# Rounded squares from ScalarE, the MLP input rounded from PSUM, a new order of work, and split products for q and k

## The reference

```python
x = x + conv31x31_depthwise(group_norm(x)) + bias
x = x + window_block(group_norm(x))

def window_block(x):            # windows of 7x7 tokens, shifted by 3
    t = windows(roll(x, (-3, -3)))                       # N, 49, 96
    h = ln(t) * ln1_s + ln1_b
    q, k, v = h @ wq + bq, h @ wk + bk, h @ wv + bv      # 12 heads of 8
    a = softmax(q k^T / sqrt(8))
    t = t + (a v) @ wo + bo
    h = ln(t) * ln2_s + ln2_b
    t = t + gelu(h @ w1 + b1) @ w2 + b2                  # 96 -> 384 -> 96
    return roll(unwindow(t), (3, 3))
```

## Time and profile before

| what | value |
|---|---|
| median of 3 runs | 5947.31 us (5946.79 to 5955.28) |
| profiled execution, its own time | 5965.81 us |
| its span, first to last instruction | 5964.0 us |
| mean granted TensorE clock | 0.976 of full speed |
| busy share of the span: PE, PEld | 94%, 74% |
| DVE, ACT, POOL | 62%, 58%, 64% |

### The profile page before, as it was taken

The page is one execution under the profiler, slowest core; times in us unless marked ns, Lnnn a source line. Parts: engine busy times, 40 slices in busy tenths (PEclk is TensorE's granted clock), DMA queues, the critical chain, the costliest instruction groups (busy, mean ns, idle before and its releaser), DMA issues.

```text
span 5964.0 us, 233920 instructions
## 1 busy us (share of the span) xinstructions
PE 5586.8 (94%) x100144; PEld 4428.8 (74%) x100144; DVE 3678.1 (62%) x6074; ACT 3454.9 (58%) x4952; POOL 3802.2 (64%) x4822
## 2 busy tenths in 40 slices
PE   6999999999959999999999999999999999999998
PEld 6999999999946666666666666666666666666665
DVE  2222222222227777777777777777777777777774
ACT  3444444444336666666666666666666666666665
POOL 2222222222247888887878888888888888788875
PEclk9999999999959999999999999999999999999997
DMA  4444444444335666666666666666666666666662
GB/s 110 108 106 106 106 107 107 106 107 106 82 84 126 140 137 136 137 139 132 137 133 139 135 138 138 138 136 136 139 138 137 135 138 138 132 138 137 134 134 58
DMA packets 1099836, 740.86 MB, mean 124 GB/s; under 512 B 465429, under 2 KB 1070709, under 8 KB 1098709
## 3 DMA queue, kind: packets, MB, share of 16 engines
q1 hardware_dynamic: 1069620, 687.18, 51.8%
q0 software_dynamic: 29184, 38.71, 2.7%
HBM read 409.02 MB, written 316.46 MB: 122 GB/s over the span
## 4 chain that ended last, share of the span: by engine, by line
POOL 34%; issue 17%; PE 8%; DVE 7%; ACT 5%; POOLq 0%; DVEq 0%; ACTq 0%
POOL b_mid_hi L715 6%; POOL b_outs L780 5%; POOL b_mid_lo L722 5%; POOL b_sq_lo L761 4%; POOL b_t_lo L754 4%; POOL b_sq_lo L729 3%; POOL b_t L745 3%; DVE b_y L990 3%; ACT b_lg L802 3%; DVE b_h L975 2%; ACT b_rstd L807 2%; PE ps_ring L1037 2%; POOL b_t_hi L750 2%; DVE b_vd L983 1%; POOL b_mx_planes L789 1%
## 5 line engine op out<-in xcount | busy, mean ns | idle before, releaser
L223 POOL TENSOR_SCALAR xn<-xin,aff 96x896 f32<-96x896 f32 x192 | 233.9, 1218 | 1207.9 <-DVE aff L330 1195.2
L1092 PEld LDWEIGHTS ps_pv<-b_vd,b_probs_t 128*64 128x64 f32 x24576 | 772.5, 140 | 163.8 <-issue 154.8
L908 DVE TENSOR_REDUCE b_mx<-ps_s 113x12 f32<-113x588 f32 x1024 | 783.4, 765 | 174.7 <-PE ps_s L1046 173.9
L815 ACT ACTIVATE b_probs_t<-ps_t 128x588 f32<-128x588 f32 x1024 | 666.9, 651 | 332.1 <-PE ps_t L1046 306.4
L417 PE MATMUL ps_conv<-toep_hi,blocks_hi 128*128 128x304 f32 (+5 forms) x4032 | 844.2, 291 | 0.0
L417 PE MATMUL ps_conv<-toep_hi,blocks_lo 128*128 128x304 f32 (+5 forms) x4032 | 839.1, 290 | 0.0
L417 PE MATMUL ps_conv<-toep_lo,blocks_hi 128*128 128x304 f32 (+5 forms) x4032 | 838.0, 289 | 0.0
L1092 PE MATMUL ps_pv<-b_vd,b_probs_t 128*64 128x18 f32 x24576 | 824.0, 213 | 0.4 <-issue 0.3
L722 POOL TENSOR_TENSOR b_mid_lo<-b_mid,b_mid_hi 128x392 fp32r<-128x392 f32 x768 | 789.8, 1028 | 22.0
L353 DVE SCALAR_TENSOR_TENSOR x1t<-ps_conv,biasb,xin 128x896 f32<-128x896 f32 x96 | 110.5, 1151 | 1024.4 <-PE ps_conv L417 1024.4
L780 POOL TENSOR_TENSOR b_outs<-b_y,b_xs 96x392 f32<-96x392 f32 x256 | 317.7, 1241 | 524.8 <-DVE b_y L990 524.8
(11 more groups left out here) (145 smaller groups left out, 12574.1 us busy)
## 6 DMA issues: line engine op xcount, KB each, us to landing
stacked_qk<-b_planes SPq DMA_DIRECT2D x512, 220.5 KB, 2.9
b_q_st<-stacked_qk SPq DMA_DIRECT2D x512, 220.5 KB, 4.4
b_k_st<-stacked_qk SPq DMA_DIRECT2D x512, 220.5 KB, 5.7
toep<-filters_padded SPq DMA_DIRECT2D x96, 936.5 KB, 6.9
stacked_qk<-b_planes SPq DMA_DIRECT2D x512, 147.0 KB, 2.3
stacked_qk<-b_planes SPq DMA_DIRECT2D x512, 73.5 KB, 1.9
b_xs<-x_scratch SPq DMA_DIRECT2D x224, 147.0 KB, 2.8
out<-b_outs SPq DMA_DIRECT2D x224, 147.0 KB, 3.2
```

What stands on the lines that cost most here:

```text
L815: act.activation(pt[:, p, 0:HEADS * TOK].rearrange("k (e n) -> k e n", e=2), ps_t[:, :, 0:HPAIR * TOK], ACT.Exp, scale=float(DH) ** -0.5). ...
L908: dve.tensor_reduce(mx[0:rows_q, :].rearrange("q (e m p) -> q e m p", e=2, p=PAIRS)[:, :, :, p], ps_s[0:rows_q, :, 0:HPAIR * TOK].rearrang ...
L1092: ins = pe.matmul(to, pt[:, p, at:at + WS], vd[:, m % VR, p, h, :, :], start=True, stop=True, skip_group_check=True)
```

## The change

1. ACT makes the rounded squares. sq1_hi and sq2_hi are written by a second Square of ACT from ps_xc; the two DVE casts go. 2. sq2_lo is subtracted by DVE, behind row_max 3, no longer by POOL. 3. h2_hi is a product that DVE reads from PSUM, ahead of h2; the cast goes. 4. The maxima's middle plane goes from DVE to POOL, as a tensor_scalar behind the output's addition and copy. 5. q and k: h1 is made twice by DVE (h1_hi, h1), then h1_lo; the weights are split once; each product is three float32r matmuls instead of one in float32, and waits for h1_lo. 6. New order: on POOL the wrap copy stands ahead of mid_hi 0, and mid_hi 1 ahead of t0; on PE below_max 2 stands between scores 1 and w1c.

```diff
@@ POOL
                 if qkv is not None:
                     pool.wait_ge(S["sq1_high"], qkv + 1)
+                    pool.wait_ge(S["sq1"], qkv + 1)
                     pool.tensor_tensor(sq1_lo[:, :], sq1[:, :], sq1_hi[:, :].bitcast(F32), ALU.subtract)
-                mid_high(mlps, 0, i)
...
                     pool.tensor_copy(xs[:, gn % XS, :, HW:XW], xs[:, gn % XS, :, 0:SHIFT])
+                mid_high(mlps, 0, i)
                 mid_low(mlps, 0)
+                mid_high(mlps, 1, i)
...
-                mid_high(mlps, 1, i)
                 mid_low(mlps, 1)
                 mid_high(mlps, 2, i)
-                if proj is not None:
-                    pool.wait_ge(S["sq2_high"], proj + 1)
-                    pool.tensor_tensor(sq2_lo[:, :], sq2[:, :], sq2_hi[:, :].bitcast(F32), ALU.subtract)
                 mid_low(mlps, 2)
...
+                if att is not None:
+                    pool.wait_ge(S["mx_rest"], att + 1)
+                    pool.tensor_scalar(mx_planes[:, 1, :, :], mx_rest[:, :, :], 1.0, 0.0, ALU.mult, ALU.add)
@@ ACT
+                if qkv is not None:
+                    square(i, qkv, sq1_hi, "xc1", "sq1_high", "sq1_split", 1.0 / C, "var1")
                 if qkv is not None:
                     square(i, qkv, sq1, "xc1", "sq1", "sq1_split", 1.0 / C)
...
                     after(act, i, "h2_done", qkv - (PROJ - QKV))
+                    after(act, i, "h2_high", qkv - (PROJ - QKV))
...
                 if proj is not None:
                     square(i, proj, sq2, "xc2", "sq2", "sq2_split")
+                if proj is not None:
+                    square(i, proj, sq2_hi, "xc2", "sq2_high", "sq2_split", used="var2")
@@ DVE
+            dve.memset(h1_hi[:, :].bitcast(F32), 1.0)
+            dve.memset(h1_lo[:, :].bitcast(F32), 0.0)
...
+            dve.tensor_copy(wqk_hi[:, :, :], wqk[:, :, :]).then_inc(S["wprep"], 1)
+            dve.wait_ge(S["wprep"], 6)
+            dve.tensor_tensor(wqk_lo[:, :, :], wqk[:, :, :], wqk_hi[:, :, :].bitcast(F32), ALU.subtract)
...
-                if qkv is not None:
-                    high(i, qkv, sq1_hi, sq1, "sq1", "var1", 1, "sq1_high")
...
                     dve.wait_ge(S["rstd1"], qkv + 1)
+                    after(dve, i, "k_ps", qkv)
+                    dve.scalar_tensor_tensor(h1_hi[0:C, :], ps_xc[0:C, 0:NT], 1.0 / C, rstd[:, :], ALU.mult, ALU.mult)
                     after(dve, i, "v_ps", qkv)
                     dve.scalar_tensor_tensor(h1[0:C, :], ps_xc[0:C, 0:NT], 1.0 / C, rstd[:, :], ALU.mult, ALU.mult)
+                    dve.wait_ge(S["h1_high"], qkv + 1)
+                    dve.wait_ge(S["h1_done"], qkv + 1)
+                    dve.tensor_tensor(h1_lo[0:C, :], h1[0:C, :], h1_hi[0:C, :].bitcast(F32), ALU.subtract)
                 row_max(i, att, 3)
                 if proj is not None:
-                    high(i, proj, sq2_hi, sq2, "sq2", "var2", 1, "sq2_high")
+                    dve.wait_ge(S["sq2_high"], proj + 1)
+                    dve.wait_ge(S["sq2"], proj + 1)
+                    dve.tensor_tensor(sq2_lo[:, :], sq2[:, :], sq2_hi[:, :].bitcast(F32), ALU.subtract)
...
+                    dve.wait_ge(S["rstd2"], proj + 1)
+                    after(dve, i, "w1_ps", NM * proj)
+                    after(dve, i, "h2_split", proj)
+                    dve.tensor_tensor(h2_hi[:, :], ps_xc[0:C, 0:NT], rstd[:, :], ALU.mult)
...
                     dve.tensor_tensor(h2[:, :], ps_xc[0:C, 0:NT], rstd[:, :], ALU.mult)
-                if proj is not None:
-                    high(i, proj, h2_hi, h2, "h2_done", "w1_ps", NM, "h2_high")
...
-                if att is not None:
-                    dve.wait_ge(S["mx_rest"], att + 1)
-                    dve.tensor_copy(mx_planes[:, 1, :, :], mx_rest[:, :, :]).then_inc(S["mx_mid"], 1)
@@ PE
                     after(pe, i, "h2_done", qkv - (PROJ - QKV))
+                    after(pe, i, "h2_high", qkv - (PROJ - QKV))
...
                 scores(i, att, 1)
+                below_max(i, soft, 2)
                 expand(i, s, mlps, 2, "w1c")
...
-                below_max(i, soft, 2)
                 scores(i, att, 2)
...
-                    pe.wait_ge(S["h1_done"], qkv + 1)
-                    product(i, s, "q", wqk[:, 0, :], h1[:, :], C, "q_ps")
+                    pe.wait_ge(S["h1_split"], qkv + 1)
+                    wait_bank(pe, i, s, "q")
+                    to = bank(i, s, "q")[0:C, 0:NT]
+                    pe.matmul(to, wqk_hi[:, 0, :], h1_hi[:, :], start=True, stop=False)
+                    pe.matmul(to, wqk_lo[:, 0, :], h1_hi[:, :], start=False, stop=False)
+                    pe.matmul(to, wqk_hi[:, 0, :], h1_lo[:, :], start=False, stop=True).then_inc(S["q_ps"], 1)
```

More of the change, by code:

```diff
@@ L498, in window_pass @@
         h1 = sb("h1", [C + 1, NT])
+        h1_hi = sb("h1_hi", [C + 1, NT], F32R)
+        h1_lo = sb("h1_lo", [C + 1, NT], F32R)
+        wqk_hi = sb("wqk_hi", [C + 1, 2, C], F32R)
+        wqk_lo = sb("wqk_lo", [C + 1, 2, C], F32R)
         h2 = sb("h2", [C, NT])
@@ L535, in window_pass @@
                  "pv_ps rden_done o_done ot_ps ot_done wo_ps t1_done xc2 sq2 var2 lg2 rstd2 h2_done w1_ps gelu_done "
-                 "w2_ps y_done added out_done sq1_high sq1_split sq2_high sq2_split h2_high h2_split").split()
+                 "w2_ps y_done added out_done sq1_high sq1_split sq2_high sq2_split h2_high h2_split h1_high h1_split").split()
         S = {n: sem("b_" + n) for n in names}
@@ L781, in step @@
                                        ALU.add).then_inc(S["added"], 1)
+                if att is not None:
+                    pool.wait_ge(S["mx_rest"], att + 1)
+                    pool.tensor_scalar(mx_planes[:, 1, :, :], mx_rest[:, :, :], 1.0, 0.0, ALU.mult, ALU.add).then_inc(
+                        S["mx_mid"], 1)
                 if mlps is not None:
@@ L816, in exps, with square @@
                                ps_t[:, :, 0:HPAIR * TOK], ACT.Exp, scale=float(DH) ** -0.5).then_inc(S["exp_done"], 1)
-            def square(i, n, dst, src, done, split, scale=1.0):
+            def square(i, n, dst, src, done, split, scale=1.0, used=None):
                 act.wait_ge(S[src], n + 1)
                 after(act, i, split, n)
+                if used:
+                    after(act, i, used, n)
                 act.activation(dst[:, :], ps_xc[0:C, 0:NT], ACT.Square, scale=scale).then_inc(S[done], 1)
@@ L910, in row_max @@
                                   ALU.max).then_inc(S["mx_done"], 1)
[L912 to L915, removed]
             def step(i, s):
@@ L945, in step @@
                     dve.wait_ge(S["rstd1"], qkv + 1)
+                    after(dve, i, "k_ps", qkv)
+                    dve.scalar_tensor_tensor(h1_hi[0:C, :], ps_xc[0:C, 0:NT], 1.0 / C, rstd[:, :], ALU.mult,
+                                             ALU.mult).then_inc(S["h1_high"], 1)
                     after(dve, i, "v_ps", qkv)
@@ L948, in step @@
                                              ALU.mult).then_inc(S["h1_done"], 1)
+                    dve.wait_ge(S["h1_high"], qkv + 1)
+                    dve.wait_ge(S["h1_done"], qkv + 1)
+                    dve.tensor_tensor(h1_lo[0:C, :], h1[0:C, :], h1_hi[0:C, :].bitcast(F32), ALU.subtract).then_inc(
+                        S["h1_split"], 1)
                 row_max(i, att, 3)
                 if proj is not None:
-                    high(i, proj, sq2_hi, sq2, "sq2", "var2", 1, "sq2_high")
+                    dve.wait_ge(S["sq2_high"], proj + 1)
+                    dve.wait_ge(S["sq2"], proj + 1)
+                    dve.tensor_tensor(sq2_lo[:, :], sq2[:, :], sq2_hi[:, :].bitcast(F32), ALU.subtract).then_inc(
+                        S["sq2_split"], 1)
                 if qkv is not None:
@@ L973, in step @@
                     dve.wait_ge(S["rstd2"], proj + 1)
+                    after(dve, i, "w1_ps", NM * proj)
+                    after(dve, i, "h2_split", proj)
+                    dve.tensor_tensor(h2_hi[:, :], ps_xc[0:C, 0:NT], rstd[:, :], ALU.mult).then_inc(S["h2_high"], 1)
+                if proj is not None:
+                    dve.wait_ge(S["rstd2"], proj + 1)
                     after(dve, i, "h2_split", proj)
                     dve.tensor_tensor(h2[:, :], ps_xc[0:C, 0:NT], rstd[:, :], ALU.mult).then_inc(S["h2_done"], 1)
-                if proj is not None:
-                    high(i, proj, h2_hi, h2, "h2_done", "w1_ps", NM, "h2_high")
                 if qkv is not None:
@@ L1135, in step @@
                 if qkv is not None:
-                    pe.wait_ge(S["h1_done"], qkv + 1)
-                    product(i, s, "q", wqk[:, 0, :], h1[:, :], C, "q_ps")
-                if qkv is not None:
-                    pe.wait_ge(S["h1_done"], qkv + 1)
-                    product(i, s, "k", wqk[:, 1, :], h1[:, :], C, "k_ps")
+                    pe.wait_ge(S["h1_split"], qkv + 1)
[4 more added lines that the diff above has]
```

(8 more changed lines are left out.)

10 lines of the change are left out of this document (7 added, 3 removed).

## The result

The changed kernel is slower: median 6097.48 us (6080.36 to 6124.23, 4 runs) against 5950.94 us, a ratio of 1.0249 with a 95% interval of 1.0212 to 1.0286. The forecast was 5847 us, faster. Most stretches of the new order came out within a quarter of a microsecond of what it said, but it missed two things: what a gap on PE does to PE's clock, and one PSUM bank.

The account below looks back on a forecast made before the run. Bound: the loop var2, ln, exp, h2, h2_hi, v copies, y, POOL's addition and queue to sq2_lo. 3.97 + 11.75 = 15.72 a step against 16.11, 0.39 x 256 = 100 us less, gave 5847 us; range 5760 to 5955.

Parts of the forecast that it names:

- var2 to y: Stretch on DVE from PE's var2 to y: 4.81 us before, 3.97 forecast with h2_hi made from PSUM, saving 0.84.
- y to POOL's mid_lo: Stretch on POOL from y to mid_lo of plane 1, now with mx_mid on POOL: 8.45 us forecast.
- var2 to h1_lo: Stretch over PE, ACT and DVE from var2 until h1_lo is ready: 12.95 us forecast, 8.98 after y.
- The lock: DVE subtractions with two SBUF inputs wait for a running POOL instruction; h1_lo, ready at 8.98, ends at 9.88 after y.
- the list of signs: Signs of being right: period 15.6 to 15.9, h1_lo rows 0.9 to 1.3, PE waiting at q, not var2.
- case C: Rival: waiting h1_lo also lets POOL's next mid_hi pass; 16.23 a step, 5978 us, slower; chance 0.15.
- DVE's subtractions for q and k stand behind sq2_lo ...; POOL's idle takes that up: DVE's subtractions and POOL's planes come some 0.5 us later after xc2; POOL's idle 1.99 before the addition absorbs it.
- case A: Main case: h1_lo waits for POOL's mid_lo, sq2_lo's wait is hidden; 15.72 us a step; chance 0.59.
- the lock missed: Rival B: neither DVE subtraction meets a POOL instruction; 15.51 us a step, 5793 us; chance 0.14.
- PE alone would allow 15.16 ...: neither is the bound: PE's own work would allow 15.16 us a step, POOL's 12.95; ACT's way to h1 and the lock bind instead.
- The rounded products: On PE, six rounded passes for q and k instead of four float32 ones: 0.16 us less a step.

Follow-up runs that it names:

- e2_no_rest_q: The changed kernel without DVE's remainder of q, so q's PSUM bank is free once ACT has read it; ratio 1.0074.
- e6_fill_xc2: The changed kernel with 3 unread matmuls on PE ahead of its wait at xc2 alone; ratio 1.0034.
- e1_qk_whole: The changed kernel with part five undone: q and k one float32 product each, no h1_hi or h1_lo; 5913.99 us, ratio 0.9903.
- e10_real_work_in_gap: The changed kernel with below_max 3 (24 matmuls) moved on PE from behind k to ahead of xc2; ratio 1.0037.
- e12_before_gap_two: The kernel before with two unread products ahead of h1 on DVE; 6273.15 us, ratio 1.0506.
- e4_before_gap: The kernel before with one unread product ahead of h1 on DVE; ratio 1.0036.
- e7_fill_var2: The changed kernel with 4 unread matmuls on PE ahead of its wait at var2 alone; 6283.69 us, ratio 1.0510.

## Why the prediction was wrong, point by point

- **var2 to y: right.** Forecast 3.97, measured 3.95 (2168.13 to 2172.08). The cast's hidden wait for POOL was real and is gone.
- **y to POOL's mid_lo: right within 0.25.** Forecast 8.45; with a period of 16.16 the mid_lo at 2164.13 stands 8.21 after y. mx_mid's row is 0.27 and stands where POOL was idle behind the addition before.
- **var2 to h1_lo: right.** Forecast 12.95, measured 12.89.
- **The lock: right in kind.** h1_lo ends 0.42 after mid_lo's row (2165.57 against 2165.15), sq2_lo too (2167.50 against 2167.08), where 0.40 was forecast from the conv pass. It cost less, since h1_lo arrived near mid_lo's end: its row is 0.71, not 0.9 to 1.3, and q started 0.73 after xc2, undelayed. PE did not wait at q for h1_lo, as the list of signs had it. The section "Who interferes with whom" of the Trainium skill's page "SBUF — State Buffer" is borne out by both rows. It is so in the whole window pass: where h1_lo (204 of 237 instances) or sq2_lo (215 of 237) starts beside a running POOL instruction, it ends 0.41 to 0.46 after that one. Behind h1_lo, POOL's next instruction ends 0.38 or more after h1_lo in all 204, so POOL never passes it. The mechanism of case C, DVE losing the lock twice, does not occur.
- **"DVE's subtractions for q and k stand behind sq2_lo ...; POOL's idle takes that up": the first step that failed.** It asked who waits for the remainders on POOL and forgot PE: var2 takes q's bank (`USES`, two banks in turn). xc2 to var2 came to 3.23 in the step shown (median 3.18), where the walk had 2.76 in case A and 2.55 with the lock missed. That is the whole difference between the 15.72 forecast and the 16.14 measured at full clock, 0.42 a step or 108 us. Run e2_no_rest_q shows the cause: without that operation PE no longer waits there. That its step is 15.72, just the forecast, is luck: xc2 to var2 is 0.25 shorter than in the walk and the rest of the step 0.26 longer. So at full clock the change is worth about nothing (e6_fill_xc2, 1.0034), not 1.7% faster.
- **"PE alone would allow 15.16 ...: neither is the bound": the step that failed most.** The walk had xc2 wait for h1, at 12.96 after var2, while PE's own work ends at 7.63 + 4.98 = 12.61. It so had a gap of 0.35 there (0.54 came) and treated it as free of charge. It is idle time with a price of its own: the clock fell 73 times, which is 2.1% or about 128 us by the difference to e6_fill_xc2. With the 108 us of the bank, that is 236 of the 250 us by which the forecast was off. None of the rivals held it. Theirs were all about the length of the path; case C had the right sign and 5978 us, for a reason that did not occur.
- The rounded products, 0.16 of PE: 2165.63 to 2166.87 is 1.24 against 1.41 before. Right within 0.01, and worth nothing here.

What stays open: why a gap of 0.6 to 0.7 ahead of var2 (e1_qk_whole, e6_fill_xc2), or even of 1.05 (e10_real_work_in_gap), brings no falls while 0.54 ahead of xc2 does. What PE does before them differs: ahead of xc2 stand small matmuls (48 of 18 columns, 24 of 49), ahead of var2 six of 392 columns and then 24 small ones. No run tests whether this makes the difference.

## What to carry to other kernels

Where an edit moves a PE wait, look not only at the length of the path but at where PE's idle time now lies: a gap of half a microsecond at one place cost 2 to 4% here through the clock, a quarter of a microsecond cost next to nothing, and cheap work put into the gap (even unread) gave the time back. The same filling at the other gap made things worse, as it took the slack that had caught the slow stretches. When an operation on the engine that reads PSUM is placed ahead of another, ask for the PSUM bank of the one behind, and go through the list of who takes that bank next. A change of several parts is best undone one by one: here two of six parts ate more than the other four gained.

## What the runs showed of the hardware that was not expected

- The granted clock went down for about 7 to 10 us at a time after a gap of 0.54 us on PE, in a kernel in which PE is at work 93% of the span. In e12_before_gap_two the gap cost about 4% through the clock, which was low for 638 of some 4000 us.
- A gap of 0.27 (e10_real_work_in_gap) left 12 falls, one of 0.12 (e4_before_gap) 3, as few as the kernel before.
- In e7_fill_var2 filling a harmless gap made things worse, 1.0510 against 1.0249: a step with a fall took 20.5 us there (mean) against 18.5, since the fill too ran at the low clock.
- A DVE subtraction with both inputs in SBUF (0.55 us when nothing holds it) that started beside a running POOL instruction ended 0.41 to 0.46 us after it (419 instances in the changed kernel). Where another POOL instruction stood right behind (204 of them), the subtraction got in first every time, and that instruction ended 0.38 or more after it.
